# Gated recurrent layer with a residual on one core: the update gate's state product placed behind the step's first three projection groups

## The reference

```python
def step(h, xs):
    xzt, xrt, xht = xs                         # x @ W_z, x @ W_r, x @ W of this step
    z = jax.nn.sigmoid(xzt + h @ U_z + vz)     # vz, vr, vh: cond @ C + b, once
    r = jax.nn.sigmoid(xrt + h @ U_r + vr)
    hh = jnp.tanh(xht + r * h @ U + vh)
    h_new = (1.0 - z) * h + z * hh
    return (h_new, h_new)
...
return x + jnp.swapaxes(out_t, 0, 1)
```

## Time and profile before

| what | us |
|---|---|
| median of 3 runs | 2264.65 (2261.95 to 2265.0) |
| the profiled execution, its own time | 2264.97 |
| span of its instructions | 2263.1 |
| PE busy in the span | 2185.4 (97%) |
| DVE, ACT, POOL busy | 1754.5, 1326.6, 687.8 |

### The profile page before, as it was taken

How to read it: one execution, slowest core, us unless ns; L and a number is a source line. 1 busy time by engine, 2 the same in 40 slices (tenths; PEclk the granted TensorE clock), 3 DMA queues, 4 the chain that set the end, 5 groups by cost and what they waited for, 6 DMA issues and landing times.

```text
span 2263.1 us, 238050 instructions
## 1 busy us (share of the span) xinstructions
PE 2185.4 (97%) x107502; PEld 1797.5 (79%) x107502; DVE 1754.5 (78%) x8226; ACT 1326.6 (59%) x4623; POOL 687.8 (30%) x1546
## 2 busy tenths in 40 slices
PE   2899999999999999999999999999999999999996
PEld 1788878888888887888888888788878888888875
DVE  5687878778778777777777777777777877877874
ACT  3566556566566665666656666556656656656652
POOL 0233333333333333333333333333333333333331
PEclk9999999999999999999999999999999999999998
DMA  9110110110110110111101101101101101101101
GB/s 196 34 38 19 38 38 19 38 37 19 38 33 23 38 35 22 38 29 28 38 24 33 38 24 32 38 19 37 38 19 38 38 19 38 38 20 38 28 11 22
DMA packets 145390, 78.48 MB, mean 35 GB/s; under 512 B 9024, under 2 KB 140608, under 8 KB 145216
## 3 DMA queue, kind: packets, MB, share of 16 engines
q1 hardware_dynamic: 145216, 76.84, 14.1%
HBM read 43.25 MB, written 33.55 MB: 34 GB/s over the span
## 4 chain that ended last, share of the span: by engine, by line
PE 95%; issue 2%; SPq 1%; DMA 1%; DVE 0%; ACT 0%; DVEq 0%; POOLq 0%; POOL 0%
PE p_bank L269 44%; PE c_bank L259 20%; PE banks L297 16%; PE banks L306 15%; SPq L152 1%; DMA x_nat<-in_x_dram 1%; SPq L147 0%; SPq L163 0%; PE p_bank L278 0%; DVE taken L631 0%; DVE state L635 0%; DVE h_t L639 0%; ACT gate_c L430 0%; SPq L155 0%; DVE h_lo L597 0%
## 5 line engine op out<-in xcount | busy, mean ns | idle before, releaser
L269 PE MATMUL p_bank<-w_hi,x_t 128*32 128x384 f16 x16384 | 1183.1, 327 | 2.4 <-issue 1.6
L269 PE MATMUL p_bank<-w_lo,x_t 128*32 128x384 f16 x8192 | 701.7, 327 | 2.2 <-issue 2.2
L269 PEld LDWEIGHTS p_bank<-w_hi,x_t 128*32 128x32 f16 x16384 | 462.3, 97 | 155.2 <-issue 1.5
L259 PEld LDWEIGHTS c_bank<-u,reset_t 128*32 128x32 f32 x32704 | 488.4, 110 | 98.6 <-DVE reset_t L611 71.7
L259 PE MATMUL c_bank<-u,reset_t 128*32 128x64 f32 x32704 | 551.0, 219 | 8.4 <-issue 8.1
L230 POOL TENSOR_TENSOR result<-x_nat,state 128x128 f32<-128x128 f32 x512 | 233.9, 457 | 1010.0 <-DVE h_lo L597 1008.4
L423 ACT ACTIVATE gate_r<-banks,gates_down 128x64 f32<-128x64 f32 x1024 | 265.6, 310 | 359.1 <-PE banks L297 358.1
L430 ACT ACTIVATE gate_c<-c_bank 128x64 f32<-128x64 f32 x1024 | 228.3, 223 | 302.8 <-PE c_bank L259 302.6
L216 POOL TENSOR_TENSOR kept<-keep,state 128x128 f32<-128x128 f32 x512 | 235.7, 460 | 551.3 <-ACT keep L426 551.3
L609 DVE TENSOR_TENSOR reset<-gate_r,state 128x64 f32<-128x64 f32 x1024 | 209.0, 204 | 209.3 <-ACT gate_r L423 205.8
L419 ACT ACTIVATE h_hi<-h_t 128x64 f16<-128x64 f32 x1024 | 261.0, 255 | 148.0 <-DVE h_t L639 80.4
(11 more groups left out here) (68 smaller groups left out, 2749.6 us busy)
## 6 DMA issues: line engine op xcount, KB each, us to landing
x_nat<-in_x_dram SPq DMA_DIRECT2D x256, 128.0 KB, 3.1
out_dram<-result SPq DMA_DIRECT2D x256, 128.0 KB, 2.8
w_stage<-in_L_cond_W_r_dram SPq DMA_DIRECT2D x4, 256.0 KB, 5.4
w_stage<-in_L_cond_W_z_dram SPq DMA_DIRECT2D x4, 256.0 KB, 8.1
w_stage<-in_L_cond_W_dram SPq DMA_DIRECT2D x4, 256.0 KB, 10.8
u<-in_L_cond_U_z_dram SPq DMA_DIRECT2D x4, 256.0 KB, 13.5
u<-in_L_cond_U_r_dram SPq DMA_DIRECT2D x4, 256.0 KB, 16.0
c_w<-in_L_cond_C_r_dram SPq DMA_DIRECT2D x4, 256.0 KB, 12.7
```

What stands on the lines that cost most here:

```text
L259: last = nc.tensor.matmul(c_bank[part(j), a, 0:N // HALVES], reset_t[:, part(q)], u[:, C, q, half_cols(j, a)], start=False, stop=q == Q - ...
L269: last = nc.tensor.matmul(p_bank[k][part(j), 0:G * N], x_t[:, c, part(q), a], w[b][:, :, q, cols(j)], start=f == 0, stop=f == GROUPS - 1, ...
```

## The change

The call of `update_product` with its signal `z_mm` is moved down on TensorE's queue. It now comes behind the wait on `c_seeded`, the `total_x` of every fourth step, the wait on `x_t_ready` and the first three groups of `project`, and directly ahead of the candidate's product. Nothing else is changed: the same instructions are issued, and the other four engines' programs are the same.

```diff
                 pe.wait_ge(seeded, now)
                 reset_product(cell(k, R), halves).then_inc(r_mm, 1)
-                update_product(cell(k, Z)).then_inc(z_mm, 1)
                 pe.wait_ge(c_seeded, now)
                 if fill:
                     if c == TOTAL_STEP and not (last and m + tt // SET >= SETS - 2):
                         total_x(TOTAL_STEP % 2, 0, 0, count(m + (tt // SET + 3)))
                     pe.wait_ge(x_t_ready, count(s + 3))
                     project(k, (c + 2) % SET, 0, BEFORE_C)
+                update_product(cell(k, Z)).then_inc(z_mm, 1)
                 if candidate_in is not None:
                     pe.wait_ge(candidate_in, 16 * J)
                 candidate_product([(reset_t_ready, a) for a in halves])
```

## The result

The changed kernel takes **2523.3 us** (median), against 2264.31 us for the kernel before on the same chip: a ratio of 1.114 [1.112, 1.117], 259 us slower. The profiled execution took 2522.36 us with a span of 2520.5 us. One of the four executions took 2837.43 us at a mean granted clock of 0.75 and is left out of the ratio; the other three lie between 2522.36 and 2523.6 us. The forecast was 2543.

A forecast was written before the change was run, and what follows sets the result against it. PE was 97% busy, but chains between engines were as long as the work covering them. A 0.72 us shift less 0.17 room gave 0.55 a step: 2264.97 + 275 + 3 = 2543 us, range 2425 to 2600.

The forecast's parts named there:

- The wait on `c_seeded`: On PE, now right behind the reset product: first projection matmul 0.23 us late, bounds 0 and 0.35.
- The third chain: Update product through `keep`, `kept`, `turn_x` to `taken`: shifted 0.72 us, 0.17 to spare, so `taken` 0.55 late.
- From `taken` to the next reset matmul: End of the step, through `h_t` and `h_hi` to PE: 1.18 us, not shortened by the change.
- The step: Time between first reset matmuls of successive steps: from 4.22 to 4.77 us, +0.55.
- Adds nothing: `total_x` on PE in one step of four: its 0.07 us were paid before too, so no added loss.
- only the third chain counts: Rival: PE passes `c_seeded` without loss; shift 0.32 us a step, 160 us, 2427 us; chance 0.08.
- only `c_seeded` counts: Rival: late `kept` holds nobody on the path; candidate's 0.23 us a step, 115 us, 2383 us; chance 0.06.
- No change: Rival: PE's work is the same and both waits fall into hidden room, 2265 us; chance 0.04.
- faster: Rival: candidate's weight loads run ahead under the update matmuls, winning 7 us, 2258 us; chance 0.02.
- The clock falls: Rival: PE idles more and its clock drops to 0.96; 0.08 us more a step, 2583 us; chance 0.04.
- `taken` waits for the very end of `turn_x`: Rival: on DVE, without the overlap, each step takes 0.07 us more, 2578 us; chance 0.05.
- the overlap at `seed_gates`: On DVE, `seed_gates` starts 0.07 us before `reset_t` ends; taken as evidence against the DRAIN rule.

The follow-up runs named there:

- `wait_only`: Kernel before, with only the wait on `c_seeded` moved ahead of the update product: 2342.69 us, 1.034.
- `seed_early`: Changed kernel, with DVE making `seed_c` between the two halves of `h_lo`: 2417.2 us, 1.067.
- `kept_late_x`: Changed kernel, with DVE waiting for `kept` only ahead of the new state and GpSimd's L203 moved ahead of `kept`: 2414.91 us, 1.066.
- `kept_late`: Changed kernel, with DVE waiting for `kept` only ahead of the first new half of the state: 2529.0 us, 1.116.
- `x_moved`: Changed kernel, with GpSimd's low part of x (L203) moved ahead of `kept`, DVE's queue as it is: 2523.98 us, 1.115.
- `all_eased`: Changed kernel, with `seed_c` between the halves of `h_lo`, DVE's wait for `kept` later and L203 ahead of `kept`: 2306.18 us, 1.0185.
- `before_all_eased`: Kernel before, update product in its old place, with the same three edits on DVE and GpSimd as `all_eased`: 2299.07 us, 1.016.
- `one_group_seed`: Changed kernel, with the update product behind one projection group and not three, and `seed_c` between the halves of `h_lo`: 2280.58 us, 1.008.

## Why the prediction was right

The time lay 20 us under the forecast, inside the range, and the mechanism was the one forecast. Point by point:

- **The wait on `c_seeded`.** Forecast: first projection matmul 0.94 us after the first reset matmul. Measured 1.03 in the step shown and 0.99 in the median one. From `seed_c`'s end it is 0.14, the sum of 0.09 and 0.05, though `wait_only` makes these parts 0.06 and 0.08. The rest lies ahead of it: `seed_c` starts 0.51 after the first reset matmul in the median step and not 0.45. It hangs on `h_lo` of the second half and starts 0.82 behind `h_hi` as before, while the first reset matmul now starts as soon as `h_hi` is there.
- **The third chain.** `keep`, `kept`, `turn_x`, `taken`: the forecast offsets 0.23, 0.44, 0.58 and 0.24 are met to the hundredth.
- **From `taken` to the next reset matmul** the forecast kept the 1.18 us of before. It is 1.07. This term was mis-sized, by -0.11, in two parts by the medians of the steps. 0.06 is the first reset matmul again: before, PE at its projection groups held it 0.37 us behind `h_hi`'s start, now it is 0.31. It comes back as the 0.06 that `seed_c` starts later after it, so these two cancel. 0.04 is a gain that I didn't foresee: a `taken` that follows `turn_x` directly, its own wait long met, has a row of 0.18 us and not 0.22, and `h_t` starts 0.50 behind it and not 0.54.
- **The step.** 4.77 forecast, 4.72 in the median step without `total_x`: 500 x -0.05 = -25 us, most of it those 0.04. With `total_x` the median step is 4.84 against 4.28 before, 0.12 over its neighbours and not 0.06. "Adds nothing" was wrong there: 125 x 0.06 = 7 us. Together they are the miss of 20 us within 2.
- **The split.** The changed kernel loses 259 us. With `c_seeded` covered (`seed_early`) 151 are left, forecast 162 as "only the third chain counts". Without the third chain's hold (`kept_late_x`, less the 36 of the second wait) some 115 are left, forecast 119 as "only `c_seeded` counts". Together that is 266 of 259: the two shifts add up, as 0.32 + 0.23 = 0.55 in the forecast does.
- **What the argument missed.** I took `taken`'s place behind `kept` in DVE's queue for the only hold. `kept_late` showed a second one of nearly the same length, L203 on GpSimd. The forecast didn't need it: the queue is the later of the two by 0.04 us, and moving L203 alone (`x_moved`) left the time as it was. Had the kernel been mended by the first reading alone, nothing would have been won.
- **PE's busy share** was forecast at 88% and is 95%: the modelled ends fill the gaps. The wait for `h_hi`, forecast at 0.3 us a step, is 0.41 on the weight loads.
- **"No change" and "faster"** are out; `all_eased` and `before_all_eased` show what they needed, every wait covered, and both are slower than the kernel before. "The clock falls" is out by the page. "`taken` waits for the very end of `turn_x`" is out by the 0.24 us. (The section of the Trainium skill's "VectorE: DVE Perf Modes" that the prediction cites there, "The DRAIN you can't avoid", adds that a next operation that isn't held starts earlier. So the prediction had that page wrong: the overlap at `seed_gates` doesn't speak against it.) No run here beats the kernel before; the nearest is `one_group_seed` at 1.008.

## What to carry to other kernels

In a recurrence whose engines hand over in a ring, an order on a full engine isn't free. Draw each result's way back to that engine, and look for room behind every result that is put later and ahead of every wait that comes earlier. Where a chain of other engines is just as long as the work that covers it, there is next to no room (here 0 to 0.17 us in a step of 4.22), and the loss is the shift less the room, times the steps.

An instruction that is late may be held twice. If one hold is removed and nothing happens, see whether the instruction's own duration has grown. Here the hold by the queue showed as a late start, and the hold by the other engine's operation as a row of double length. Look as well whether the edit has put an instruction of its own into the chain: here it hid a part of the gain.

## What the runs showed that I had not expected

- A VectorE operation with two SBUF inputs (128x64, fp32) took 0.46 us in place of 0.23 while GpSimd's `tensor_tensor` on SBUF ran; a VectorE transpose beside the same operation kept its 0.31.
- A second wait ahead of `state` cost 0.07 us though it had long been met: the wait for `taken` then stands in a semaphore instruction of its own, and `state` came 0.33 us behind `taken` and not 0.26, 36 us over the run.
- The same holds on TensorE: a wait carried by a register instruction let the first matmul go 0.14 us after the producer's end; carried by the matmul itself it was 0.06.
- `total_x` took 0.10 to 0.12 us of TensorE's queue right behind the reset product, and 0.06 behind the update product.
